# Negated maxima and image-prompt probabilities turned by VectorE and placed by SyncE's transfers

## The reference, cut to what matters

```python
# B = 8 batches, S = 512 queries, D = 320, C = 512, 20 heads of 16
# context of 1601 tokens: the last 8 are image-prompt tokens, 1593 are text
q = split_heads(x @ w_q, 20)
k = split_heads(text @ w_k, 20);      v = split_heads(text @ w_v, 20)
out_text = merge(softmax(q @ k.T / 4) @ v)                 # 1593 keys
k_ip = split_heads(ip @ w_k_ip, 20);  v_ip = split_heads(ip @ w_v_ip, 20)
out_ip = merge(softmax(q @ k_ip.T / 4 + mask_ip) @ v_ip)   # 8 keys, mask from boxes
return (out_text + out_ip) @ w_out + b_out + x
```

## Time and profile before

| what | value |
|---|---|
| time of three runs, median (lowest to highest) | 1902.52 us (1896.72 to 1904.98) |
| the profiled execution: its time, its span | 1900.24 us, 1897.8 us |
| PE busy | 1853.3 us (98% of the span) |
| DVE, ACT, POOL busy | 1332.1 us (70%), 1202.6 us (63%), 301.4 us (16%) |
| mean granted TensorE clock | 0.987 |
| chain that ended last | PE 92%, DVE 3%, issue 2%, DMA 2% |

### The profile page before, as it was taken

How to read it: one execution, slowest core, us unless ns; L and a number is a source line. 1 busy time by engine, 2 the same in 40 slices (tenths; PEclk the granted TensorE clock), 3 DMA queues, 4 the chain that set the end, 5 groups by cost and what they waited for, 6 DMA issues and landing times.

```text
span 1897.8 us, 43032 instructions
## 1 busy us (share of the span) xinstructions
PE 1853.3 (98%) x17984; PEld 747.7 (39%) x17984; DVE 1332.1 (70%) x1673; ACT 1202.6 (63%) x2368; POOL 301.4 (16%) x358
## 2 busy tenths in 40 slices
PE   6999999999999999999999999999999999999998
PEld 2343344343444434443444434434344343444332
DVE  5777776677776777778676777767777677767871
ACT  1066666666666666666666666666666666666675
POOL 5012111111111111111111111112111111111000
PEclk8898999999999999999999999999999999999999
DMA  8335434464443634436344453436344364443410
GB/s 218 64 77 130 90 69 83 75 164 77 79 88 73 164 72 74 85 69 166 71 86 83 83 151 68 82 69 163 71 77 91 67 168 80 73 84 70 89 29 23
DMA packets 91627, 175.29 MB, mean 92 GB/s; under 512 B 37193, under 2 KB 60682, under 8 KB 87594
## 3 DMA queue, kind: packets, MB, share of 16 engines
q1 hardware_dynamic: 83018, 141.47, 39.7%
q0 software_dynamic: 5872, 29.11, 4.2%
q10 hardware_dynamic: 2544, 1.97, 0.3%
HBM read 117.57 MB, written 48.82 MB: 88 GB/s over the span
## 4 chain that ended last, share of the span: by engine, by line
PE 92%; DVE 3%; issue 2%; DMA 2%; POOL 1%; SPq 0%; ACT 0%; POOLq 0%; DVEq 0%
PE pv_bank L750 25%; PE max_bank L686 21%; PE work_bank L528 12%; PE work_bank L561 11%; PE exp_bank L734 9%; PE work_bank L577 3%; PE work_bank L539 3%; PE max_bank L697 2%; DVE tile_max L1018 1%; PE exp_bank L738 1%; DVE tile_max L1025 1%; PE work_bank L567 1%; PE work_bank L551 0%; DMA ctxt<-in_ctx_t 0%; PE work_bank L588 0%
## 5 line engine op out<-in xcount | busy, mean ns | idle before, releaser
L921 ACT ACTIVATE probs<-exp_bank 128x512 f32<-128x512 f32 x1896 | 995.5, 598 | 441.2 <-PE exp_bank L734 431.3
L1025 DVE TENSOR_REDUCE tile_max<-max_bank 128x2 f32<-128x1024 f32 x632 | 773.9, 1225 | 414.0 <-PE max_bank L686 409.0
L686 PE MATMUL max_bank<-k_stack,q_stack 48*128 48x512 f32 x1896 | 562.4, 466 | 13.9 <-DVE tile_max L1025 11.1
L750 PE MATMUL pv_bank<-probs,v_ones 128*17 128x512 f32 x3840 | 517.0, 602 | 0.1
L1027 DVE TENSOR_REDUCE tile_max<-max_bank 128x1 f32<-128x512 f32 x632 | 430.1, 681 | 0.0
L734 PE MATMUL exp_bank<-q_stack,k_stack 50*128 50x512 f32 x1896 | 409.9, 401 | 0.8 <-ACT probs L921 0.8
L686 PEld LDWEIGHTS max_bank<-k_stack,q_stack 48*128 48x128 f32 x1896 | 234.7, 185 | 399.8 <-issue 256.7
L528 PE MATMUL work_bank<-ctxt,wk 128*32 128x400 f32 x2496 | 251.9, 509 | 8.3 <-DMA wk<-in_w_k 5.4
L561 PE MATMUL work_bank<-wv,ctxt 128*32 128x320 f32 x3072 | 253.3, 439 | 0.4 <-ACT s_ip L950 0.4
L734 PEld LDWEIGHTS exp_bank<-q_stack,k_stack 50*128 50x128 f32 x1896 | 236.9, 187 | 39.8 <-ACT probs L921 28.1
L561 PEld LDWEIGHTS work_bank<-wv,ctxt 128*32 128x32 f32 x3072 | 93.1, 110 | 167.9 <-issue 108.4
(11 more groups left out here) (115 smaller groups left out, 824.1 us busy)
## 6 DMA issues: line engine op xcount, KB each, us to landing
k_stack<-scratch_k SPq DMA_DIRECT2D x240, 200.0 KB, 8.7
scratch_k<-k_parts SPq DMA_DIRECT2D x80, 400.0 KB, 4.7
ctxt<-in_ctx_t POOLq DMA_DIRECT2D x28, 800.0 KB, 7.6
q_stack<-scratch_q SPq DMA_DIRECT2D x240, 64.0 KB, 2.3
scratch_q<-q_parts SPq DMA_DIRECT2D x80, 128.0 KB, 10.0
r_wide<-scratch_r SPq DMA_DIRECT2D x39, 256.0 KB
xres<-in_x SPq DMA_DIRECT2D x8, 640.0 KB, 6.9
out<-xres SPq DMA_DIRECT2D x32, 160.0 KB, 2.0
```

The costliest lines, as they stand in the source:

```text
L686: nc.tensor.matmul(round_place(n, r)[:, k, :], exact(q_stack[stack, slot, c, t * 128:(t + 1) * 128]), exact(k_stack[stack, slot, c, chunk ...
L750: last = nc.tensor.matmul(pv_bank[h * 32:h * 32 + VW, :], v_ones[:, v_slot(b, kt), head * VW:(head + 1) * VW], p, start=(kt == 0), stop=(k ...
L921: nc.scalar.activation(dst, exp_place(group_no, at), ACT.Exp, scale=SCALE).then_inc(probs_ready, 1)
L1025: nc.vector.reduce_max(flat[:, at:at + 2], place[:, 0:2, :], AX.X).then_inc(max_taken, 1)
```

## The change

The three kinds of identity product (L610, L657, L663) and ScalarE's copies after them are gone. VectorE turns `neg_parts` in 32x32 blocks with one instruction at the end of `negative_parts`, and `p_ip` with four instructions (one for each query tile) at g = 2, v = 12 to 15. A block turned in place leaves the four groups of 32 queries on four groups of partitions. SyncE puts them together: eight transfers for each group of heads (two sides by four blocks) for the maxima, in place of ScalarE's two, and 20 transfers for each batch (four blocks by five) for the probabilities. `o_t[:, 3]` keeps another order of queries, which the OUT products read with another slice.

Around it, `normalise` moves from SyncE to GpSimd, cut in two and put between the splits; the reciprocals are taken at v = 4 instead of v = 2. The load of the next context waits for the loads of a stack, no longer for the maxima. At the start GpSimd makes `kip_own` ahead of the splits of group 1.

```diff
+NEG_LOADS = SIDES * 4
+IP_LOADS = 4 * (HEADS * IPT // 32)
+BLOCK = 32
+TURNED = HEADS * IPT // BLOCK
...
     if last:
-        put(3, ("TA",), 4, (12, 4))
-        put(3, ("TB",), 4, (13, 4))
...
-    else:
-        put(3, ("TA",), 4, (16, 4))
-        put(4, ("TB",), 4, (16, 4))
...
-SCALE_AT = (2, 2, 1, 1, 1)
-INVERT_AT = 2
-SOFTMAX_AT = (4, 5, 6, 9, 10, 11)
+TURN_AT = (12, 13, 14, 15)
+INVERT_AT = 4
+SOFTMAX_AT = (3, 5, 6, 9, 10, 11)
...
+            def pack_ip(b):
+                sp.wait_ge(ip_turned, (b + 1) * QT)
+                for a in range(128 // BLOCK):
+                    rows = slice(a * BLOCK, (a + 1) * BLOCK)
+                    for j in range(TURNED - 1):
+                        sp.dma_start(o_t[j * BLOCK:(j + 1) * BLOCK, 3, a * 128:(a + 1) * 128],
+                                     p_turned[rows, j, :, :].rearrange("p t n -> p (t n)")).then_inc(ip_packed, 16)
+                    sp.dma_start(o_t[64:96, 2, :].rearrange("p (t a n) -> p a t n", t=QT, n=BLOCK)[:, a, :, :],
+                                 p_turned[rows, TURNED - 1, :, :]).then_inc(ip_packed, 16)
+            def send_negatives(group_no):
+                sp.wait_ge(negs_turned, group_no + 1)
+                for side in range(SIDES):
+                    row, at = side * SIDE + STACK, side * PARTS * PAIRS
+                    for a in range(128 // BLOCK):
+                        place = q_stack[row:row + PARTS, group_no % RING, :, :].rearrange("p c (t a n) -> p a (c t) n", t=QT, n=BLOCK)
+                        sp.dma_start(place[:, a, :, :], neg_turned[a * BLOCK + at:a * BLOCK + at + PARTS * PAIRS, :])\
+                          .then_inc(neg_loaded, 16)
...
-                    if group_no:
-                        normalise(group_no - 1)
...
+                    if g == 3:
+                        pack_ip(b)
                     if group_no and g != 1:
                         pack(group_no - 1, (g - 1) % NG, None)
+                    if g == 2:
+                        send_negatives(group_no + 1)
                     if group_no + 3 < B * NG:
                         store_k(group_no + 3)
                     if g == 1:
...
                                 store_out(b - 1, t, number(("OUT", t)))
+                    if g != 2 and group_no + 1 < B * NG:
+                        send_negatives(group_no + 1)
...
-            def negative_piece(group_no):
-                pe.wait_ge(neg_step, group_no * 3 + 3)
-                nc.tensor.matmul(work_bank[0:NEGS, 0:128], neg_parts[:, :], ident_f[:, :], start=True, stop=True)\
-                  .then_inc(work_full, 1)
...
+                nc.vector.transpose(neg_turned[:, :], neg_parts[:, :]).then_inc(negs_turned, 1)
...
+            def turn_ip(b, t):
+                dve.wait_ge(ip_step, b * 5 + 5)
+                nc.vector.transpose(p_turned[:, :, t, :], p_ip[:, t, :].rearrange("p (j n) -> p j n", n=BLOCK)).then_inc(ip_turned, 1)
...
+                                if piece[1] == NG:
+                                    dve.wait_ge(ip_packed, (b + 1) * IP_LOADS * 16)
                                 ip_scale(piece[1], number)
...
-            for c in range(2):
-                split_k(1, c, PRO_ORDER["K", 1, c])
             pool.wait_ge(consts_loaded, 80)
             pool.wait_ge(work_empty, PRO_ORDER["KIP",] + 1)
             own_k(0)
+            for c in range(2):
+                split_k(1, c, PRO_ORDER["K", 1, c])
```

More of the change, by code:

```diff
@@ L149, in work_order @@
         for v in range(VISITS):
-            if v == NEG_AT and not (last and g == NG - 1):
-                order["NEG", g + 1] = len(order)
             piece, turn = plan.get((g, v), (None, None))
@@ L165 @@
 PRO_PLAN += [(("V", t), half, 1) for t in range(8) for half in HALVES] + [(("V", 8), HALVES[0], 1), (("V", 8), HALVES[1], 0)]
-PRO_PLAN += [(("NEG", 0), ALL, 0)] + [(("K", 2, c), half, 1 - c * n) for c in range(2) for n, half in enumerate(HALVES)]
+PRO_PLAN += [(("K", 2, c), half, 1 - c * n) for c in range(2) for n, half in enumerate(HALVES)]
 assert sum(n for _, _, n in PRO_PLAN) == ROUNDS + LEAD
@@ L244, in cross_attention @@
         neg_parts = sb("neg_parts", [128, NEGS])
-        neg_rows = sb("neg_rows", [NEGS, 128])
+        neg_turned = sb("neg_turned", [128, BLOCK])
         zero = sb("zero", [128, 1])
@@ L571, in v_piece, with ip_or_heads @@
                     last.then_inc(work_full, 1)
+            def ip_or_heads(k, t, at, rows):
+                first = at // BLOCK * 128 + t * BLOCK if k == 3 else t * 128 + at
+                return slice(first, first + rows)
             def out_piece(t, k_range, bank=work_bank[:, 0:D], k_end=3):
@@ L830, in body @@
                                 exp_tile(group_no, at)
-                        if v == NEG_AT and group_no + 1 < B * NG:
-                            pe.wait_ge(work_empty, work_number(b, ("NEG", g + 1), first, last))
-                            negative_piece(group_no + 1)
                         kt = PV_AT.get(v)
@@ L892, in v_copy @@
                     last.then_inc(work_empty, 1)
-            def negative_copy(group_no, number, first_group):
-                act.wait_ge(work_full, number + 1)
-                if not first_group:
-                    act.wait_ge(neg_loaded, group_no * 32)
-                rows = NEGS
-                copy(neg_rows[:, :], work_bank[0:rows, 0:128]).then_inc(work_empty, 1)
-                act.wait_ge(work_empty, number + 1)
-                for side in range(SIDES):
-                    first_row = side * SIDE + STACK
-                    act.dma_start(q_stack[first_row:first_row + PARTS, group_no % RING, :, :],
-                                  neg_rows[side * (rows // SIDES):(side + 1) * (rows // SIDES), :]).then_inc(neg_loaded, 16)
             def exp_tile(group_no, at):
@@ L956, in _ @@
                     v_copy(0, piece[1], number)
-                elif piece[0] == "NEG":
-                    negative_copy(0, number, True)
             def body(b, first, last):
@@ L968, in body @@
                             o_copy(group_no - 1)
-                        if v == NEG_AT and group_no + 1 < B * NG:
-                            negative_copy(group_no + 1, work_number(b, ("NEG", g + 1), first, last), False)
                         if (g, v) == (2, 8):
```

79 lines of the change are left out of this document (38 added, 41 removed).

## The result

| | before | changed |
|---|---|---|
| median of six runs each (lowest to highest) | 1902.94 us (1896.72 to 1908.89) | 1965.91 us (1962.73 to 1972.61) |
| ratio, 95% interval | | 1.0338 (1.0308 to 1.0367) |
| profiled execution: its time, its span | 1900.24 us, 1897.8 us | 1966.53 us, 1964.7 us |
| mean granted TensorE clock | 0.987 | 0.971 |

What follows compares the result with a forecast made beforehand. TensorE, busy for 98% of the span, was taken as the bound. The terms summed as 1900.2 - 14.4 - 2.0 + 31.9 + 25.6 + 5.0 = 1946.3 us, taken as 1946, with a range of 1908 to 1980.

Steps and rivals of the forecast that it cites:

- everything late: Rival: g = 3 stalls by 5 us and the earlier context load slows landings in g = 1; 1971 us, chance 0.12.
- TA and TB: TensorE's products turning the probabilities, in g = 3 and g = 4: removing them gains 14.4 us, 0.99 each for fourteen.
- The maxima's identity product costs nothing: At v = 14, VectorE's drain of `max_bank` sets the time, so removing this product (16.4 us busy) saves nothing there.
- The start: First maxima without the product's detour, and `kip_own` made earlier: net gain 2.0 us, bounds 0 and 3.4.
- g = 1: Eight transfers behind SyncE's pack and stores: seven stalls of 3.3 us plus 1.25 us of clock each, together 31.9 us.
- g = 3: Maxima behind twenty transfers, pack and keys on SyncE: seven stalls of 2.4 us plus 1.25 us of clock, 25.6 us.
- The end: Last but one group's `normalise` on GpSimd's queue, 4 us, and the last g = 3 stall, 1 us: together 5 us.
- The load of the context "was not waited for": The context's load starts some 12 us earlier and was not waited for; no cost counted.
- "Elsewhere `normalise` has 30 us of room": Moving `normalise` to GpSimd, away from the end of the kernel: 30 us of room, no cost counted.
- only g = 1 stalls: Rival: SyncE reaches the maxima of g = 3 in time because its loads come earlier; 1920.7 us, chance 0.20.
- Not slower: Rival: SyncE issues at 0.44 us, the clock stays up over stalls, g = 3 is on time; 1900.5 us, chance 0.15.
- The identity products do count: Rival: without the maxima's products TensorE's time at v = 14 falls by 15.6 us; 1931 us, chance 0.03.

Runs made afterwards that it cites:

- e5: Changed kernel with the maxima back on TensorE's identity product and ScalarE's two transfers, context's wait left as changed: 1886.15 us, ratio to before 0.9914.
- e12: e5 with the identity product of the maxima issued twice in each of 40 places: 1888.94 us, ratio to before 0.9939.
- e2: Changed kernel with SyncE sending the turned maxima ahead of pack and stores in g = 1 alone: 1926.64 us, ratio to before 1.0132.
- e1: Changed kernel with SyncE sending the turned maxima first in both g = 1 and g = 3: 1891.53 us, ratio to before 0.9942.
- e10: e5 with `normalise` of the last but one group alone issued by SyncE again: 1887.07 us, ratio to before 0.9924.
- e3: Changed kernel with the maxima back on the identity product and the context's load waiting for the maxima again: 1975.68 us, ratio to before 1.0386.
- e6: e1 with `normalise` back on SyncE and the reciprocals at v = 2 again: 1993.77 us, ratio to before 1.0478.
- e4: Changed kernel with the probabilities turned by TensorE's products TA and TB again, maxima still turned and sent last: 1936.49 us, ratio to before 1.0177.

## Why the prediction was right, and which sizes were off

The forecast was 1946 us and slower; it is 1966 and slower, inside the range of 1908 to 1980. It is 20 us short, and the rival *everything late*, 1971, came nearer by number. Of its signs nearly all came: seven waits at the first tile of g = 2 of 3.1 to 4.4 us, seven of 2.4 to 4.0 at that of g = 4, issues over 0.6 us, a landing of 1.7 us, 2.53 us from L706 to L695, and a lower clock behind all but one stall. By its own steps:

- **TA and TB**: 14.4 us predicted. The g = 3 and g = 4 of e5 give 12.1. It isn't TB that was taken too large: g = 3, which TA leaves, gains 0.84 us in each batch, and g = 4, which TB leaves, 0.89. The 0.99 between two starts was more than the queue gets back for either.
- **The maxima's identity product costs nothing**: right, within 0.03 us a group. L706 to L695 is 2.53 us in the changed kernel (975.43 to 977.96) as in the earlier trace rows, and doubling the product in e12 costs 0.02 to 0.22 us a group for 0.38 us more of its busy time.
- **The start**: 2.0 us predicted. The first exponential tile comes at 91.6 in place of 96.4 here. Over all kernels it comes at 91.4 to 94.3 with turned maxima (six kernels, mean 92.7) and at 92.6 to 97.1 with the product (eight, mean 95.1): 2.3 us, less than either group is wide. The idle time moved as foreseen: TensorE waits 12.5 us for `k_stack`, until 47.6. GpSimd's new order at the start has no run of its own.
- **VectorE's transpositions**: 0.2 us and under 0.5 predicted, 0.21 and 0.33 measured, both hidden.
- **g = 1**: the mechanism was right in each link, the size too small: 7 x (3.3 + 1.25) = 31.9 us against 7 x (3.78 + 1.84) = 39.3. SyncE came to the maxima 5.0 us after VectorE's last part on average (5.2 in the rows shown), not 4.5, because the pack took 2.5 to 3.8 us to issue, mean 3.1, and not 2.48 each time: in four batches one of its four issues takes 1.5 to 2.0 us in place of 0.59. It did so before as well (3.72 us in batch 2, 3.43 in batch 7), but the prediction read a single end. Why is open; the context's load isn't the reason in batch 7, which has the longest pack and no such load. The issues took 0.66 us each, not 0.62, and the landing 1.7, not 2.0, which nearly cancel. The larger miss is the clock, 1.25 put down, 1.84 measured; the bound of 1.7 was nearer than the value taken.
- **g = 3**: 25.6 us predicted, 35.1 measured from e2 to e1, and 36.6 by the groups g = 3 and g = 4 of the changed kernel and e5 (646.9 and 610.3). Up to the end of the keys the timing held: counted from the moment at which TensorE wants the tile, the pack and the keys were to end 2.6 to 4.7 us ahead of it, and ended 4.9 us ahead (978.09 and 982.98). The step that failed is the next: 6.3 us from there to the landing, where the trace has 8.2, since the first two issues right behind the keys' 400 KB take 1.34 and 1.74 us. The stalls are 3.28 us on average in place of 2.4, and g = 4, where the clock behind them stands, is 1.85 us longer than g = 4 of e5 from its first tile to L706, in place of 1.25.
- **g = 4 on time**: no stall for the maxima there but one of 0.1 us, right.
- **The end**: 5 us predicted. The wait for `o_t` grew by 0.8 us, the last g = 3 stalls by 2.6, and the last batch and the end give about 4.7 (11.0 us more than before, less the 6.3 that the last g = 1 takes). That agrees by luck as much as by reason, since like kernels differ by up to 7 us in these groups (164.3 in e5, 171.4 in e10). Of GpSimd's part, 4 us taken from one landing beside much traffic, e10 shows 2.6. The estimate of 1.2 us from the figures of the Trainium skill ("DMA: Bandwidth & Descriptors", section "Specifications") was too low and the 4 too high.
- **The load of the context "was not waited for"**: right for this kernel, but it hid how much hangs on it. It starts 17 us earlier against the first tile of g = 2 (19.7 us ahead of where TensorE wants it, 2.7 before), not 12. e3, which is e5 with only this wait put back, is 90 us slower.
- **"Elsewhere `normalise` has 30 us of room"**: right, and again only half of it. The prediction has the move as free room for SyncE. e6 shows what else hangs on it: with `normalise` back on SyncE and the reciprocals back at v = 2, VectorE waits 64.2 us for the twenty transfers.

Of the rivals, *only g = 1 stalls* fell with the seven stalls of g = 3. *Everything late* had 5 us for a stall of g = 3, where 3.28 were measured, and landings in g = 1 slowed by the context's load, where the landing was 0.3 us shorter than forecast; it came near by its number, not by its mechanism. *Not slower* needed 0.44 us for an issue; none of the maxima's was under 0.61. *The identity products do count* fell with L706 to L695 and e12.

## What to carry to other kernels

Cheap work taken from a full engine is worth only what its place in the schedule shows: 16 us of identity products were all but free beside a drain, while fourteen pieces of 1 us without cover were worth 12 us. When many small transfers take its place, count each as about 0.65 us of the issuing queue, read every repetition of the place and not one, ask what stands behind them there and which buffers they read, and send first what is wanted first; the same transfers in another order made 74 us of difference. Pieces of a change that look like padding (a wait moved, a helper's transfers moved to another queue) may be what holds it together: take them back one at a time before calling them free.

## What the runs showed of the chip

- A stall costs more than its idle time: 39.3 us were paid for 26.4 us of waits, 1.8 us on top of each. Behind fourteen of fifteen stalls, 2.6 to 4.4 us long, TensorE ran at 1.2 GHz until 3.4 to 6.4 us after the tile's start. The length of the stall alone doesn't decide it: there was no such stretch behind one of 2.4 us, nor behind one of 3.1 us in e4 (645.66), and there was one behind 2.1 us in e2 (1659.14).
- The issue of a transfer isn't a constant: 0.62 to 0.66 us from one to the next on SyncE between SBUF tiles, with 2 to 32 KB each. Right behind 400 KB the first two of eight took 1.34 and 1.74 us and the rest 0.61. With 4.2 us in between, at the ends of g = 4, the eight took 5.3 us as elsewhere.
- GpSimd's queue took 2.6 us more than SyncE's for three small transfers in a chain. By the Trainium skill ("DMA: Bandwidth & Descriptors", section "Specifications") an estimate gives 1.2 us. The measured figure is the one to use.
- In the last batch, with VectorE nearly as busy as TensorE, the granted clock of two like kernels was 1.00 and 0.50 over the same 10 us. Nine runs of one of them spread over 15 us with their mean clock (0.985 to 0.994). What decides it stays open.
